# Stores of the strip pooling and strip filter stages issued channel by channel from ScalarE's queue, with a fourth matrix slot

## The reference

```python
x = x + L0(gn(x))   # attention over 8x8 windows, keys and values sampled bilinearly at learned offsets
x = x + L1(gn(x))   # 3x3 convolution of rounded, clipped values
x = x + L2(gn(x))   # 8x8 block DCT, divided by a table, rounded, clipped
x = x + L3(gn(x))   # strip pooling, 1x1 mix, strip filters

# L3
s = pool_strip(x, gp) + pool_strip(x, lp7, 7) + pool_strip(x, lp11, 11)  # means along rows, then columns
out = einsum('nchw,oc->nohw', s, spec_w) + spec_b
x1, x2 = split(out, 2, axis=1)
o1 = cubic(x1, w11h, w11w, gb11, 11)   # 11 taps along a row, then along a column; taps from a sigmoid of the image's mean
o2 = cubic(x2, w7h, w7w, gb7, 7)       # gb[0] * filtered + gb[1] * input
```

## Time and profile before

| | |
|---|---|
| median of 3 runs | 28332.71 us (28328.62 to 28334.44) |
| the profiled execution | 28324.44 us, its span 28322.6 us |
| PE busy | 21072.8 us, 74% |
| PEld busy | 17803.4 us, 63% |
| DVE busy | 16079.4 us, 57% |
| ACT busy | 11402.1 us, 40% |
| POOL busy | 17378.3 us, 61% |
| mean granted clock of TensorE | 0.849 of full speed |

### The profile page before, as it was taken

The page is one execution under the profiler, slowest core; times in us unless marked ns, Lnnn a source line. Parts: engine busy times, 40 slices in busy tenths (PEclk is TensorE's granted clock), DMA queues, the critical chain, the costliest instruction groups (busy, mean ns, idle before and its releaser), DMA issues. The chain is left out here.

```text
span 28322.6 us, 349873 instructions
## 1 busy us (share of the span) xinstructions
PE 21072.8 (74%) x123212; PEld 17803.4 (63%) x123212; DVE 16079.4 (57%) x28104; ACT 11402.1 (40%) x28980; POOL 17378.3 (61%) x16423
## 2 busy tenths in 40 slices
PE   2668867787678866788677876688677886778778
PEld 2567655676566765676556764677556765567666
DVE  6676457744576347654577446763576445763442
ACT  2444434434344334434344334534345343443331
POOL 0677557756677557766577566775577565775500
PEclk9779977898779977898779987799778987799886
DMA  6647554655546555566546555466445655465555
GB/s 210 164 116 213 171 139 127 176 178 175 144 117 200 169 146 133 147 197 176 136 127 190 165 170 141 118 208 178 135 130 167 182 173 141 121 199 165 153 176 160
DMA packets 2408270, 4551.90 MB, mean 161 GB/s; under 512 B 568544, under 2 KB 1602272, under 8 KB 2258272
## 3 DMA queue, kind: packets, MB, share of 16 engines
q1 hardware_dynamic: 1881936, 3437.67, 40.6%
q0 software_dynamic: 524288, 1074.79, 14.8%
q10 hardware_dynamic: 272, 16.78, 0.2%
HBM read 2943.64 MB, written 1600.65 MB: 160 GB/s over the span
## 5 line engine op out<-in xcount | busy, mean ns | idle before, releaser
L1214 POOL DMA_INDIRECT at_G<-table,at_idxg x16384 | 17267.8, 1054 | 8554.6 <-issue 4922.8
L1252 ACT ACTIVATE at_E<-at_S,at_mx 128x64 f32<-128x64 f32 x16384 | 4057.2, 334 | 2521.2 <-DVE at_mx L1361 2515.5
L1308 PE MATMUL kc_attention<-kc_ident,at_M 128*128 128x128 f32 x16384 | 2866.0, 347 | 2100.7 <-DVE at_M L1369 2100.6
L1308 PEld LDWEIGHTS kc_attention<-kc_ident,at_M 128*128 128x128 f32 x16384 | 2701.0, 257 | 2276.4 <-issue 2273.6
L1396 DVE SCALAR_TENSOR_TENSOR at_x<-kc_attention,kc_pb,at_x 128x256 f32<-128x256 f32 x1024 | 495.3, 484 | 5849.3 <-PE kc_attention L1333 5627.1
L1299 PE MATMUL kc_attention<-at_vals,at_PT 128*128 128x68 f32 x16384 | 2384.4, 307 | 913.0 <-DVE at_S L1353 685.6
L1299 PEld LDWEIGHTS kc_attention<-at_vals,at_PT 128*128 128x128 f32 x16384 | 2319.3, 224 | 1074.6 <-issue 701.1
L1258 ACT ACTIVATE at_KM<-kc_attention,kc_headmask 128x256 f32<-128x256 f32 x4096 | 1604.9, 474 | 3429.0 <-PE kc_attention L1308 3428.8
L1369 DVE TENSOR_TENSOR at_M<-at_G,at_wtsc 128x2048 f32<-128x2048 f32 x1024 | 2343.2, 2288 | 896.8 <-DMA at_G<-table,at_idxg 893.3
L361 PE MATMUL kc_ring<-kc_wkv,tb_xn 128*128 128x256 f32 x9216 | 2267.9, 394 | 330.8 <-DVE tb_T L377 274.0
L1323 PE MATMUL kc_attention<-at_KM,at_Qm 128*128 128x256 f32 x8192 | 2237.3, 422 | 196.9 <-ACT at_KM L1258 196.2
(11 more groups left out here) (226 smaller groups left out, 33211.9 us busy)
## 6 DMA issues: line engine op xcount, KB each, us to landing
table<-tb_T SPq DMA_DIRECT2D x2304, 256.0 KB
pl_mt<-pool_matrices SPq DMA_DIRECT2D x576, 660.0 KB
at_G<-table,at_idxg POOLq DMA_INDIRECT x16384
cv_xr<-x_padded SPq DMA_DIRECT2D x288, 640.0 KB
st_x<-in_x SPq DMA_DIRECT2D x288, 512.0 KB, 7.8
tb_x<-in_x SPq DMA_DIRECT2D x288, 512.0 KB
x<-cv_x SPq DMA_DIRECT2D x288, 512.0 KB
dc_x<-x SPq DMA_DIRECT2D x576, 256.0 KB
```

Source lines behind the costliest of these rows:

```text
L1214: pool.indirect_dma_start(self.G[n % 2][:, i, :, :].rearrange("p a c -> p (a c)"), None, entries[i % HEADS], bass.IndirectOffsetOnAxis(ap= ...
L1252: last = act.activation(self.E[:, p, h, p2, :], self.S[:, p, h, p2, :], ACT.Exp, bias=self.mx[:, i:i + 1])
L1308: mm = pe.matmul(self.kt_ps[:, p * P:(p + 1) * P], self.M[:, corner, 0, p * 2 * HEADS:(p + 1) * 2 * HEADS, :].rearrange("p n d -> p (n d)" ...
```

## The change

In both stages the stores move from SP's program into ACT's, one channel at a time, each behind ACT's own copy of a later channel: in `pl` the store of channel `k - 2` behind the copies of channel `k`, in `fi` the store of channel `k - 3` behind the copy of channel `k`. ACT waits for `so_ready` or `f_used` of that channel ahead of the store. SP keeps the loads. In `pl` its block loads get a place of their own between the matrix loads, and the matrix tile gets a fourth slot. In `fi` SP loads channel by channel, each load waiting for the channel that lay in its place 8 channels ago, where it had waited for a block. What DVE and PE do, and what DVE waits for ahead of a block, is as before.

```diff
+POOL_SLOTS = 4
@@ stage_pool
-    mt = m.sb("mt", [P, MATRIX_SLOTS, MATRIX])
+    mt = m.sb("mt", [P, POOL_SLOTS, MATRIX])
...
         def load_matrices(k):
-            if k >= MATRIX_SLOTS:
-                sp.wait_ge(s_ready, k - MATRIX_SLOTS + 1)
-            sp.dma_start(mt[:, k % MATRIX_SLOTS, :], pm[k, :, :]).then_inc(m_loaded[k % MATRIX_SLOTS], 16)
-
-        for n in range(NB + 3):
-            if n < NB:
-                yield n * NC4 - 3.5
-                if n > 1:
-                    sp.wait_ge(s_ready, (n - 1) * NC4)
-                for j in range(NC4):
-                    sp.dma_start(x[:, n % 2, j, :]..., channel_rows(x3, n * NC4 + j)).then_inc(x_loaded[n % 2], 16)
-                for j in range(NC4):
-                    yield n * NC4 + j - 1.7
-                    load_matrices(n * NC4 + j)
-            if n >= 2 and n < NB + 2:
-                o = n - 2
-                yield (o + 1) * NC4 + 1.8
-                sp.wait_ge(so_ready, (o + 1) * NC4)
-                for j in range(NC4):
-                    sp.dma_start(channel_rows(s_d, o * NC4 + j), so[:, o % 2, j, :]...).then_inc(so_stored[o % 2], 16)
+            if k >= POOL_SLOTS:
+                sp.wait_ge(s_ready, k - POOL_SLOTS + 1)
+            sp.dma_start(mt[:, k % POOL_SLOTS, :], pm[k, :, :]).then_inc(m_loaded[k % POOL_SLOTS], 16)
+
+        def load_block(n):
+            if n > 1:
+                sp.wait_ge(s_ready, (n - 1) * NC4)
+            for j in range(NC4):
+                sp.dma_start(x[:, n % 2, j, :]..., channel_rows(x3, n * NC4 + j)).then_inc(x_loaded[n % 2], 16)
+
+        yield -3.5
+        load_block(0)
+        for k in range(C):
+            yield k - 1.7
+            load_matrices(k)
+            if k % NC4 == NC4 - 2 and k // NC4 + 1 < NB:
+                yield k - 1.5
+                load_block(k // NC4 + 1)
 
     def scalar(act, pos, after):
-        for k in range(C):
-            yield k + .5
...
+        for k in range(C + 2):
+            if k < C:
+                yield k + .5
...
             if k > 1:
+                o = k - 2
+                yield k + .6
+                act.wait_ge(so_ready, o + 1)
+                act.dma_start(channel_rows(s_d, o), so[:, o // NC4 % 2, o % NC4, :]...).then_inc(so_stored[o // NC4 % 2], 16)
@@ stage_filter
     def sync(sp, pos, after):
-        for n in range(NB + 3):
-            if n < NB:
-                yield n - 1.2
-                if n > 1:
-                    sp.wait_ge(zx_ready, (n - 1) * NC4)
-                    sp.wait_ge(t_ready, (n - 1) * NC4)
...
-            if n >= 3:
-                b = n - 3
-                yield b + 1.75
-                sp.wait_ge(f_used, (b + 1) * NC4)
-                for j in range(NC4):
-                    sp.dma_start(channel_rows(outv, b * NC4 + j), o[:, b % 2, j, :]...).then_inc(stored[b % 2], 16)
+        def load_channel(k):
+            if k >= 2 * NC4:
+                sp.wait_ge(zx_ready, k - 2 * NC4 + 1)
+                sp.wait_ge(t_ready, k - 2 * NC4 + 1)
+            for dst, src in ((z, z_d), (x, x3)):
+                sp.dma_start(dst[:, k // NC4 % 2, k % NC4, :]..., channel_rows(src, k)).then_inc(loaded[k // NC4 % 2], 16)
...
+        for k in range(C - 2 * NC4):
+            yield k / NC4 + .2
+            load_channel(k + 2 * NC4)
 
     def scalar(act, pos, after):
+        for k in range(C + 3):
...
+            if k > 2:
+                b = k - 3
+                yield k / NC4 + .2
+                act.wait_ge(f_used, b + 1)
+                act.dma_start(channel_rows(outv, b), o[:, b // NC4 % 2, b % NC4, :]...).then_inc(stored[b // NC4 % 2], 16)
```

More of the change, by code:

```diff
@@ L755, in stage_pool @@
     x_loaded = [m.sem(f"x_loaded{i}") for i in range(2)]
-    m_loaded = [m.sem(f"m_loaded{i}") for i in range(MATRIX_SLOTS)]
+    m_loaded = [m.sem(f"m_loaded{i}") for i in range(POOL_SLOTS)]
     y_ready = m.sem("y_ready")
@@ L761, in stage_pool @@
     so_stored = [m.sem(f"so_stored{i}") for i in range(2)]
-    filters = lambda k, which: mt[:, k % MATRIX_SLOTS, which * 4 * BAND:(which + 1) * 4 * BAND].rearrange("p (a i b) -> p a i b", a=2, i=2)
-    columns = lambda k, which: mt[:, k % MATRIX_SLOTS, 8 * BAND + which * P:8 * BAND + (which + 1) * P]
+    filters = lambda k, which: mt[:, k % POOL_SLOTS, which * 4 * BAND:(which + 1) * 4 * BAND].rearrange("p (a i b) -> p a i b", a=2, i=2)
+    columns = lambda k, which: mt[:, k % POOL_SLOTS, 8 * BAND + which * P:8 * BAND + (which + 1) * P]
     near = (slice(0, BAND), slice(P - REACH, W))
@@ L794, in scalar @@
         begin(act, after)
-        for k in range(C):
-            yield k + .5
+        for k in range(C + 2):
+            if k < C:
+                yield k + .5
+                if k > 1:
+                    act.wait_ge(s_ready, k - 1)
+                for wc in range(2):
+                    act.wait_ge(y_ready, 2 * k + wc + 1)
+                    act.activation(Y[:, k % 2, wc, :, :].rearrange("p i n -> p (i n)"), ring[:, wc, :], ACT.Copy).then_inc(y_copied, 1)
             if k > 1:
[L798 to L801, removed]
+                o = k - 2
+                yield k + .6
+                act.wait_ge(so_ready, o + 1)
+                act.dma_start(channel_rows(s_d, o), so[:, o // NC4 % 2, o % NC4, :].rearrange("p (s w) -> p s w", s=2)).then_inc(so_stored[o // NC4 % 2], 16)
     def tensor(pe, pos, after):
@@ L1039, in sync @@
         begin(sp, after)
[L1040 to L1055 removed]
+        def load_channel(k):
[3 more added lines that the diff above has]
+            for dst, src in ((z, z_d), (x, x3)):
+                sp.dma_start(dst[:, k // NC4 % 2, k % NC4, :].rearrange("p (s w) -> p s w", s=2), channel_rows(src, k)).then_inc(loaded[k // NC4 % 2], 16)
+        for k in range(2 * NC4):
+            if k == NC4:
+                yield -.2
+            load_channel(k)
+        for k in range(C - 2 * NC4):
+            yield k / NC4 + .2
+            load_channel(k + 2 * NC4)
         yield NB + 2
@@ L1060, in scalar @@
     def scalar(act, pos, after):
[L1061 to L1066, removed]
+        outv = out[bass.ds(pos["image"], 1), :, :, :].rearrange("a c h w -> (a c) h w")
+        for k in range(C + 3):
+            if k < C:
+                yield k / NC4 + .17
+                act.wait_ge(t_ready, k + 1)
+                if k > 1:
+                    act.wait_ge(f_ready, k - 1)
+                act.activation(U[:, k % 2, :, :], bank(max(2 * k - 1, 0)), ACT.Copy).then_inc(u_ready, 1)
+            if k > 2:
+                b = k - 3
+                yield k / NC4 + .2
+                act.wait_ge(f_used, b + 1)
+                act.dma_start(channel_rows(outv, b), o[:, b // NC4 % 2, b % NC4, :].rearrange("p (s w) -> p s w", s=2)).then_inc(stored[b // NC4 % 2], 16)
     def tensor(pe, pos, after):
```

5 lines of the change are left out of this document (2 added, 3 removed).

## The result

The changed kernel takes 26112.35 us (median of 4 runs, 26068.24 to 26145.37), before 28330.67 us. The ratio is 0.9216, 95% interval 0.9200 to 0.9232. The direction and the mechanism were right, but the gain was larger than forecast: 2218 us between the medians, and 2179 us between the two profiled executions (28324.44 and 26145.37 us), where I had 1777. The step that failed is the time of a block of the strip filters beside the attention, 19.9 us forecast and 17.3 measured; it is taken up behind the experiments.

What follows compares the result with a forecast made beforehand. PE bounds pooling, and DVE's waits for late stores leave holes and a low clock in both stages. Gains of 1776 beside the attention and 131 alone, less 78 and 52, give 1777 us: about 26550 us, range 26,200 to 27,050.

Steps and rivals of the forecast that it cites:

- the time of a block of the strip filters beside the attention: Strip filters beside the attention: a block falls from 27.9 to 19.9 us, the time of the clean block.
- The mechanism and the waits: Both stages: timely stores end DVE's waits for pooled and out, 1190 and 1193 us, to under 30 and under 100.
- the clock in both stages: Sign in pooling and filters beside the attention: granted clock over 0.95, from 0.92 and 0.82.
- PE's waits for ACT: Sign: PE's waits for ACT's copies stay under 10 us a stage despite the added stores.
- the signs named ahead: Predicted profile: short store waits, pooling about 540 us a pass, filters about 315, clock over 0.95, ACT issues about 0.5 us.
- the length of the filters: Sign: the strip filters beside the attention take about 315 us a pass.
- The rule that issuing from several engines only saves issue time: Store issue: by this rule alone the gain is SP's issue time, on no path, so 0; held not to decide.
- Pooling beside the attention: Strip pooling beside the attention: a block falls from 41.4 to 33.0 us, gaining 8.4 x 14 = 118 us a pass.
- Filters beside the attention: Strip filters beside the attention: a block falls by 8.0 us to 19.9, gaining 8.0 x 13 = 104 us a pass.
- The floor that I had worked out: Strip filters beside the attention: POOL's gathers need 21.7 us a group, 16.3 us a block; gain bound 151 us a pass.
- ScalarE and what was left of the waits: Deductions: 78 us for 1152 store issues on ACT, 52 us for 0.5 us of waiting left per filter block.
- The last image: Stages running alone: pooling gains 8.5 x 14 = 119 us; filters, at clock 0.52, only 12 us of holes.

Runs made afterwards that it cites:

- e3: The kernel before with three block slots for pl_so and fi_o instead of two, stores still on SyncE four at a time; 26189.31 us, ratio 0.9245.
- e4: The changed kernel with its channel stores put back on SyncE, behind the matrix or channel loads; 26200.90 us, ratio 0.9241.
- e5: The changed kernel with every channel store cut into four, 4608 issues on ScalarE instead of 1152; 26208.56 us, ratio 0.9257.
- e11: The kernel before with eight extra matmuls on PE ahead of the last image's strip filters; 28310.81 us, ratio 0.9993.
- e2: The kernel before with only the strip filter stage changed, strip pooling as before; 27125.35 us, ratio 0.956.
- e9: The changed kernel run again without any edit, for its median and a second trace of the last image's filters; 26068.11 us, ratio 0.9215.

## Why the forecast was too small

**The mechanism and the waits** held. The store waits are 0 and 0, the clock in both stages is 0.97 or more, PE's waits for ACT are 2.5 us in pooling, and e3 and e4 show that the lateness of the stores is the cause of all but some 90 us. Of the signs named ahead, only the length of the filters is off: 277 us a pass where I had 315. The rule that issuing from several engines only saves issue time (the Trainium skill, "DMA: Bandwidth & Descriptors", section "Issuing engines are not separate DMA queues") agrees with e4, where SyncE does nearly as well (26201 us against 26112). Read as a forecast of no gain for this change it would have failed by 2218 us, because the gain is in when a store is issued.

**Pooling beside the attention**: 8.4 us a block forecast, measured (538.2 - 437.1) / 13 = 7.8. A block takes 33.6 us where I took 33.0. In the mean of the eight passes the stage gained 107.4 us: in all 859 us where I had 944, 85 too many.

**Filters beside the attention**: this is the step that failed. I took 19.9 us a block, the one clean block (one without a store wait) of the earlier trace rows, where the blocks now take 225.3 / 13 = 17.3. The block ends of the filters in the trace after come 19.9, 14.9, 16.4 and 16.0 us apart, and again 19.9, 14.9 and so on, with some 20 and 21 us for blocks 9 and 10: four blocks go with three groups of the attention, and the second block is a long one in every pass. I had measured one phase of a cycle of four and applied it to all. The trace before had the warning in it: no store wait falls into the last block either, right behind the windows of the earlier trace rows, and that block took 16.3 us (DVE's last steps of blocks 15 and 16 end at 13780.3 and 13796.6 us). The floor that I had worked out and used only as a bound, 16.3 us from POOL's gathers, was near; with the gather's measured 1088 ns it is 0.75 x 22.3 = 16.7. The stage gained 142.4 us a pass in the mean, and I had 104: 8 x 38.4 = 307 us too few before the terms below.

**ScalarE and what was left of the waits**: I took off 78 us for the issues and 52 for what was left of the waits. The waits are zero, so the 52 were wrong. Of the issues, e5 bounds 1152 at 42 us, and the gains of the stages below hold whatever they cost. Together up to 130 us too few.

**The last image**: pooling gained 126 us (I had 119). The filters gained 82 (I had 12), because the clock rose in the middle of the stage and stayed. I had taken the low clock there for a fixed property of the stage, and the store wait as harmless behind it. Both kernels come out of the low clock after a while, and only in the kernel before does a store wait throw it back (e11, and the trace before at 241 us into the stage). The size of this gain is luck in part: by the traces of the stage it can be 38 us (e2) or 165 (e9).

The sum: 1777 - 85 + 307 + 130 + 7 + 70 = 2206, against 2179 measured; the other 27 us were lost outside these stages, and I have not placed them. The 307 is the largest term, but alone it would have put the forecast at 26,240, still some 130 us above the measured time; the terms for ScalarE, the rest of the waits and the last image make up the remainder.

## What to carry to other kernels

A double buffer whose store is issued late stalls the engine that fills it, and whoever waits for that engine, even where the transfer itself is short: look at what stands ahead of the store in its queue, and either move it or add a slot. When a stall on PE goes, count the clock behind it too, from the granted clock of stretches with and without it. And when a clean stretch is taken as the price of all, take one whole cycle of everything that runs beside it, and check it against the floor of the next engine, here POOL's gathers.

## What the runs showed of the hardware that I had not expected

- TensorE can be busy for over 200 us and stay at the 1.2 GHz level: 266.6 us in e2, above. In the profiled execution of the changed kernel the last filters ran 176 us at a granted clock of 0.5 with PE busy throughout (20.8 us a block of four channels), then at 1.0 (10.7 us a block). In another execution of the same program they had the full clock after 5 us.
- A store's issue on ScalarE took 0.366 us alone, and with four in a row (e5) 0.617 us in the median for `pooled` (up to 1.99) and 0.492 for `out`. On SyncE the four of a block took 2.77 us. One channel of `pooled` at a time landed in 2.9 us, four at once in 5.5.
- The gathers on GpSimd got slower in the filters: 209.95 / 193 = 1088 ns each at 220 GB/s, where it was 190.40 / 191 = 997 ns before at 147 GB/s. In pooling they did not: 334.13 / 341 = 980 ns at 188 GB/s, 333.33 / 342 = 975 ns before at 157. So a denser traffic alone does not explain it, and the cause is open.
